# Weights in three groups, the first image's rows ahead of them, and new turn strings in a sixteen-image, four-block kernel

## The chip, the cores and the metric

The kernel runs on one core of a Trainium2 chip. The metric is the device time of one execution in microseconds (us). Before the change it was 2970.29 us, the median of three runs (2969.28 to 2974.66).

## The reference

Sixteen images of 256 rows by 128 features, all in float32, go through four branches one after the other. Each branch takes a layer norm of the image, scales and shifts it by rows of a modulation computed once from a condition vector, and adds its result back, for the first two branches and the second two times a gate row:

```
mod = (silu(c) @ wmod).reshape(16, 6, 1, 128)       # once for each of two layers
h = layernorm(x) * (1 + ca) + sa
x = x + ga * mamba(h)                 # branch a: conv of 4 taps, selective scan over 256 steps, 16 states
x = x + gb * routed(h2)               # branch b: 8 small experts, 2 chosen, and a shared one
x = x + ga1 * delta_rule(h3)          # branch c: 8 heads, gated delta rule over 256 steps
x = x + gb1 * attention_and_8_experts(h4)           # branch d
```

The images do not depend on each other. The weights are the same for all.

## The kernel before, in words

One image is too serial to fill the engines, so two are in work at a time. The steps of an image are split into a FIRST_HALF (x: branches a, b and the projections of c) and a SECOND_HALF (y: the pair products, the triangular inversion and the application of c, and branch d). `follow` writes, for each engine, first the whole first half of image 0, then a loop over i = 1 to 15 whose body holds the first half of image i and the second half of image i-1, and at the end the second half of image 15. In the loop body the order of the steps on each engine is a string of x and y, one string for each of TensorE (PE), VectorE (DVE), ScalarE (ACT) and GpSimd (POOL), in the table TURNS: each letter takes the next step of that half which this engine has. The engines run their own rows in order and meet through semaphores; a step that waits holds back everything behind it on its engine.

The steps that the change and the prediction speak of, with their lines in the kernel before:

- First half, branch a. `a_norm`/`a_norm2`: layer norm (DVE L1211 to L1223, one power on POOL L513). `a_turn`: transpose on PE (L797) and scale and shift on ACT (L602). `a_in`: the two input products (PE L808, L811), copied by ACT (L607, tanh L609). `a_conv`: 4 taps on DVE (L1278, L1281). `a_zgate` (L1271), `a_silu2` (L1286), `a_xproj` (PE L817, L819; ACT L618, L619), `a_split` (DVE L1291 to L1300), `a_dt` (PE L826), `a_soft` and `a_step` (DVE L1306 to L1315, ACT L623, L625). Then the scan in 8 groups: `a_scan` st is a spread of B and C on PE (L832), 4 exponentials on ACT (L637), the product `drive` (DVE L1324) and the scan itself (DVE L1336); `a_read` st is the product with C (DVE L1344), a sum on POOL (L535) and a product that adds up on PE (L855). `a_out` is the output product (PE L861), `a_res` the residual (DVE L1232, L1234).
- Second half, pair products: four groups of `c_logd` (PE L960, L961, ACT L704) and two `c_prod` (PE L970, DVE L1484, L1486); POOL builds `c_gmask` (L555). Then the inversion: `c_first` (DVE L1494), and five levels of `lev_T` (DVE L1500, L1503), `lev_Z` (PE L978, DVE L1507), `lev_TT` (PE L978, ACT L715), each for two chunks of the image. Then its application (`c_top`, `c_low`, `c_X` and so on), branch d, and its experts `d_up` (PE L1141, ACT L762), `d_down` (PE L1151) and `d_mix` (DVE L1632).

In the program's names, `wide` and `small` hold branch a's values, `mats` and `inv` the pairs and the inversion, `pad` the padded rows of a convolution, `banks` is PSUM, where products land.

Before the first image there is a prologue. SyncE (SP) issues all 43 weight loads with one semaphore, `loaded` (L450). All other engines wait for all of it. Then ACT and DVE make silu(c), PE makes the modulation from it (L780, L783), DVE turns it into `shift_scale` (L1179, L1182) and into gate rows (L1188 to L1200), SP stores the gate rows to DRAM (L452), waits for that, and only then loads the first image (L456) and the gate rows spread over the partitions (L459).

## Time and profile before

| what | value |
|---|---|
| median of 3 runs | 2970.29 us |
| the profiled execution's own time | 2970.33 us |
| its span, first to last instruction | 2968.5 us |
| PE busy | 2431.9 us, 82% |
| DVE busy | 2207.0 us, 74% |
| ACT busy | 1202.5 us, 41% |
| POOL busy | 650.6 us, 22% |
| mean granted TensorE clock | 0.907 of 2.4 GHz |

In the timeline, the pair stage of the loop starts at 201.94 us for image 1, at 377.56 and at 555.19 us for the next ones, so a pass of the loop takes some 177.6 us. A pass can be read in stretches of a few microseconds: what the engines do there, how much of it they are busy, and which of them is waited for. A total over the span hides these.

### The profile page before, as it was taken

The numbers are of one execution on the slowest core, as the hardware profiler recorded it, in microseconds if no ns is written. First come the engines' busy times: TensorE is split into PE (matmuls) and PEld (weight loads), VectorE is DVE, ScalarE is ACT, GpSimd is POOL, SyncE is SP. The second block draws the span as 40 slices with busy tenths as digits, with TensorE's granted clock in tenths as the row PEclk, the third lists the DMA queues.
The fourth block names the chain that finished last, engine by engine and source line by source line (L and its number), as shares of the span: only waits on it lengthen the run. The fifth ranks groups of instructions, "written<-read, shape, count | busy, mean of one in ns | idle before, by whom it ended". The sixth has DMA issues, their size and how long they took to land.

```text
span 2968.5 us, 60546 instructions
## 1 busy us (share of the span) xinstructions
PE 2431.9 (82%) x22424; PEld 1916.4 (65%) x22424; DVE 2207.0 (74%) x5056; ACT 1202.5 (41%) x2697; POOL 650.6 (22%) x465
## 2 busy tenths in 40 slices
PE   1478878979887897978889887887988789798897
PEld 1166766757666585756757676675866667576685
DVE  1668777787977778787787877778697777878752
ACT  0333532435344253533525353343534425353432
POOL 0222122131212212122132212213121221312110
PEclk9569989989899998989989998998989899898999
DMA  4000000000000000000000000000000000000000
GB/s 125 2 2 3 1 7 3 7 3 7 2 3 7 3 7 3 1 8 2 8 3 7 2 3 7 3 7 3 7 2 3 7 3 7 3 3 5 1 6 2
DMA packets 24830, 21.39 MB, mean 7 GB/s; under 512 B 7217, under 2 KB 21570, under 8 KB 24530
## 3 DMA queue, kind: packets, MB, share of 16 engines
q1 hardware_dynamic: 24530, 17.26, 2.1%
q8 instruction: 204, 3.34, 0.5%
q14 instruction: 96, 0.79, 0.1%
HBM read 15.13 MB, written 2.13 MB: 6 GB/s over the span
## 4 chain that ended last, share of the span: by engine, by line
PE 42%; issue 27%; DVE 23%; POOL 5%; ACT 2%; SPq 1%; DMA 1%; DVEq 0%; POOLq 0%; ACTq 0%
PE banks L978 6%; PE banks L1151 4%; PE banks L1004 4%; PE banks L1141 4%; PE banks L855 4%; DVE wide L1336 3%; PE banks L970 3%; DVE wide L1324 3%; DVE wide L1344 2%; PE banks L996 2%; PE banks L918 2%; PE banks L960 2%; POOL lg L539 2%; DVE inv L1507 2%; PE banks L927 2%
## 5 line engine op out<-in xcount | busy, mean ns | idle before, releaser
L535 POOL TENSOR_TENSOR wide<-wide 128x512 f32<-128x512 f32 x128 | 260.2, 2033 | 861.0 <-DVE wide L1344 543.5
L1456 DVE SCALAR_TENSOR_TENSOR wide<-pad,conv,wide 128x256 f32<-128x256 f32 x864 | 368.6, 494 | 0.0
L637 ACT ACTIVATE wide<-small,a_neg 128x255 f32<-128x255 f32 x512 | 217.7, 496 | 188.0 <-DVE wide L1336 187.9
L1336 DVE TENSOR_TENSOR_SCAN wide<-wide 128x1024 f32<-128x1024 f32 x128 | 291.6, 2278 | 1.9 <-ACT wide L637 0.3
L762 ACT ACTIVATE inv<-banks,up1b 128x256 f32<-128x256 f32 x512 | 212.1, 489 | 126.6 <-PE banks L1141 126.4
L1141 PE MATMUL banks<-inv,up 128*128 128x256 f32 x1024 | 262.3, 387 | 0.0
L1151 PE MATMUL banks<-down,inv 128*128 128x128 f32 x2048 | 258.9, 277 | 0.0
L1151 PEld LDWEIGHTS banks<-down,inv 128*128 128x128 f32 x2048 | 248.7, 192 | 5.0
L832 PE MATMUL banks<-bc,sel3b 96*128 96x256 bf16 x512 | 110.4, 323 | 162.5 <-DVE wide L1344 134.3
L978 PE MATMUL banks<-inv 64*64 64x64 f32 x5120 | 200.9, 237 | 48.1 <-DVE inv L1507 44.3
L978 PEld LDWEIGHTS banks<-inv 64*64 64x64 f32 x5120 | 184.8, 151 | 73.7 <-issue 73.6
L996 PE MATMUL banks<-hideb,identb 128*128 128x512 bf16 x640 | 207.2, 408 | 0.0
L978 PE MATMUL banks<-inv,mats 64*64 64x64 f32 x5120 | 186.3, 229 | 11.0 <-DVE inv L1500 6.6
L978 PEld LDWEIGHTS banks<-inv,mats 64*64 64x64 f32 x5120 | 174.2, 144 | 32.5 <-issue 30.0
L832 PEld LDWEIGHTS banks<-bc,sel3b 96*128 96x128 bf16 x512 | 45.0, 111 | 230.8 <-DVE wide L1344 149.9
L1141 PEld LDWEIGHTS banks<-inv,up 128*128 128x128 f32 x1024 | 181.2, 190 | 19.4
L715 ACT COPY inv<-banks 128x512 f32<-128x512 f32 x160 | 92.7, 579 | 216.5 <-DVE inv L1503 199.9
L1324 DVE TENSOR_TENSOR wide<-banks,small 128x1024 f32<-128x1024 f32 x128 | 154.0, 1203 | 7.7 <-PE banks L832 7.6
L513 POOL TENSOR_TENSOR vscale<-vscale,expo 128x16 f32<-128x16 f32 x16 | 46.3, 2896 | 512.1 <-DVE rq L1465 512.1
L1344 DVE TENSOR_TENSOR wide<-banks,wide 128x1024 f32<-128x1024 f32 x128 | 154.9, 1210 | 1.1
L602 ACT ACTIVATE hT_x<-banks,shift_scale 128x256 f32<-128x256 f32 x48 | 27.1, 565 | 295.3 <-PE banks L797 295.3
L927 PEld LDWEIGHTS banks<-ones_col,wide 128*128 128x128 f32 x1024 | 137.4, 200 | 14.2 <-issue 8.2
(277 smaller groups left out, 4966.3 us busy)
## 6 DMA issues: line engine op xcount, KB each, us to landing
gates_bc<-gate_rows SPq DMA_DIRECT2D x32, 128.0 KB, 2.9
up<-in_W SPq DMA_DIRECT2D x1, 2048.0 KB
x<-in_x SPq DMA_DIRECT2D x16, 128.0 KB, 2.2
out<-xn_y SPq DMA_DIRECT2D x16, 128.0 KB, 2.1
wide<-in_wmod SPq DMA_DIRECT2D x2, 384.0 KB
con<-in_con SPq DMA_DIRECT2D x1, 724.0 KB
w_k<-in_Wk SPq DMA_DIRECT2D x1, 512.0 KB
w_q<-in_Wq SPq DMA_DIRECT2D x1, 512.0 KB
```

What stands on the lines that cost most here:

```text
L535: g.tensor_tensor(ypart[p % 2], r[:, 0:512], r[:, 512:1024], ALU.add).then_inc(a_yp.h, 1)
L637: last = s.activation(decay[st % 2][:, at + 1:at + T], dt[:, c, 1:T], ACT.Exp, scale=a_neg[:, c, st * SG + q:st * SG + q + 1])
L762: s.activation(hm[e % 2][:, m, :], bank(3 + half, T, q * T), ACT.Relu, bias=up1b[:, HB1 * e + m:HB1 * e + m + 1]).then_inc(d_hid.h, 1)
L927: last = t.matmul(bank(2, 1, (kind * TILES + ch) * NH + m), sq[m % 2][:, kind, ch * P:(ch + 1) * P], ones_col[:], start=True, stop=True)
L978: last = t.matmul(PS[a:b, out, h * HALF:(h + 1) * HALF], weights(h, a, b), values(h, a, b), start=True, stop=True)
L996: t.matmul(bank(bk), identb[:], hideb[:].unsqueeze(1).broadcast_to([P, HG, P]), start=True, stop=True)
L1141: last = t.matmul(bank(3 + half, T, q * T), up1[:, e, m * P:(m + 1) * P], xxT, start=True, stop=True)
L1151: last = t.matmul(bank(bk, D, j * D), hm[e % 2][:, m, j * P:(j + 1) * P], down1[:, HB1 * e + m, :], start=m == 0, stop=m == HB1 - 1)
L1324: v.tensor_tensor(drive[st % 2].rearrange("p (q c t) -> p q c t", q=SG, c=CB), bank(0).rearrange("p (q t) -> p q t", t=T).unsqueeze(2).bro ...
L1336: v.tensor_tensor_scan(state[st % 2], decay[st % 2], drive[st % 2], 0.0, ALU.mult, ALU.add).then_inc(a_h.h, 1)
L1344: v.tensor_tensor(r, bank(1).rearrange("p (q t) -> p q t", t=T).unsqueeze(2).broadcast_to([P, SG, CB, T]), r, ALU.mult).then_inc(a_rd.h, 1)
L1456: v.scalar_tensor_tensor(dst, src, w, dst, ALU.mult, ALU.add).then_inc(c_conv.h, 1)
```

## The change

Weights come in three groups with a semaphore each: `loaded` (the condition, the constants and the modulation's weights, and between them, with its own semaphore, the first image), `loaded_first` (what the first steps of branch a need) and `loaded_late` (the rest, the larger part). Each engine waits for the group it needs at the place where it needs it: PE waits for `loaded_late` ahead of image 0's `a_out`, DVE ahead of its `a_res`, ACT ahead of its first `c_proj`. The gate rows are computed after the first image's layer norm, and POOL's memsets stand ahead of its wait. The four turn strings are other ones.

```diff
-    "tensor": ("yyyyyyyyyyyyxxyyyyyyxyyxyyyyyyxxxyxxyyxxyyyyxx...
+    "tensor": ("yyyyyxyxyyyyyyxyyxyyyyyyyyxyyyyxxxxyyxxyyyxyyx...
...
-            (con[:], a["con"]), (cT[:, 0, :], a["c0T"]), (cT[:, 1, :], a["c1T"]),
+            (cT[:, 0, :], a["c0T"]), (cT[:, 1, :], a["c1T"]), (con[:], a["con"]),
             (wmod[:, 0, :], a["wmod0"]), (wmod[:, 1, :], a["wmod1"]),
+        ]
+        loads_first = [
...
+            for dst, src in loads[:2]:
+                sp_.dma_start(dst, src).then_inc(loaded, 16)
+            load_x(0)
+            for dst, src in loads[2:]:
+                sp_.dma_start(dst, src).then_inc(loaded, 16)
+            for dst, src in loads_first:
+                sp_.dma_start(dst, src).then_inc(loaded_first, 16)
+            for dst, src in loads_late:
+                sp_.dma_start(dst, src).then_inc(loaded_late, 16)
             sp_.wait_ge(prep_dve, 12)
             sp_.dma_start(gates_dram, gates[:]...).then_inc(gates_stored, 16)
             sp_.wait_ge(gates_stored, 16)
-            load_x(0)
             load_gates(0, 0, gx_loaded)
...
             s.activation(xc[:, 0, 0:2 * NB]..., cT[:], ACT.Exp, scale=-1.0).then_inc(silu_c, 1)
+            s.wait_ge(loaded_first, LOADED_FIRST)
...
-            s.wait_ge(prep_dve, 12)
+            s.wait_ge(prep_dve, 8)
...
-            t.wait_ge(prep_dve, 12)
-            t.wait_ge(prep_act, 7)
             t.wait_ge(prep_pool, 1)
+            t.wait_ge(loaded_first, LOADED_FIRST)
...
+            def a_norm2(i):
+                norm2(i, 0)
+                if isinstance(i, int):
+                    modulation()
+                    gate_rows()
```

On DVE, in the prologue and the first steps of image 0, these rows stand in a row before, where `shift_scale` and `gates` are the modulation, `stats_x` and `mv_x` the layer norm:

```order
L1177 TENSOR_TENSOR cT<-cT,small 128x32
L1179 COPY shift_scale<-banks 128x128
L1182 TENSOR_SCALAR shift_scale<-shift_scale 128x16 x4
L1188 TENSOR_SCALAR inv<-banks 16x512
L1189 TENSOR_SCALAR inv<-banks 16x512
L1191 TENSOR_SCALAR inv<-banks 16x512
L1194 TENSOR_TENSOR inv<-inv 16x512
L1195 TENSOR_SCALAR inv<-inv 16x512
L1197 TENSOR_TENSOR gates<-inv 16x512
L1200 TENSOR_SCALAR gates<-gates 16x128
L1211 BN_STATS stats_x<-x 128x6 x2
```

and these now (L1239 to L1251 are the layer norm, L1206 the copy of the modulation):

```order
L1200 TENSOR_TENSOR cT<-cT,small 128x32
L1239 BN_STATS stats_x<-x 128x6 x2
L1241 COPY carried<-con 128x1
L1243 BN_AGGR mv_x<-stats_x 128x2 x2
L1245 TENSOR_SCALAR mv_x<-mv_x 128x2
L1251 TENSOR_SCALAR xn_x<-x,mv_x 128x128 x2
L1206 COPY shift_scale<-banks 128x128
L1209 TENSOR_SCALAR shift_scale<-shift_scale 128x16 x4
L1217 TENSOR_SCALAR inv<-banks 16x512
L1218 TENSOR_SCALAR inv<-banks 16x512
```

The layer norm has moved ahead of the modulation's copy, while PE makes the modulation; the gate rows stay between it and image 0's convolution.

On PE, in the pair stage of the loop, the end of the stage was (L960, L961 is a `c_logd`, each L970 pair a `c_prod`, L797 `a_turn`, L808 and L811 `a_in`):

```order
L957 REGISTER_ALU
L960 MATMUL banks<-inv,con 128x512
L961 MATMUL banks<-hideb,identb 128x512
L967 REGISTER_ALU
L970 MATMUL banks<-kq 128x256 x2
L967 REGISTER_ALU
L970 MATMUL banks<-kq 128x256 x2
L795 ISA
L797 MATMUL banks<-con,xn_x 128x128 x2
L808 MATMUL banks<-hT_x,w_in 128x256 x2
L811 MATMUL banks<-hT_x,w_in 128x256 x2
L982 ISA
```

and the second of the four groups is now (L983, L984 for `c_logd`, L993 for `c_prod`, L817 for `a_turn`, L828 and L831 for `a_in`):

```order
L980 REGISTER_ALU
L983 MATMUL banks<-inv,con 128x512
L984 MATMUL banks<-hideb,identb 128x512
L990 ISA
L993 MATMUL banks<-kq 128x256 x2
L815 ISA
L817 MATMUL banks<-con,xn_x 128x128 x2
L990 REGISTER_ALU
L993 MATMUL banks<-kq 128x256 x2
L828 MATMUL banks<-hT_x,w_in 128x256 x2
L831 MATMUL banks<-hT_x,w_in 128x256 x2
L980 REGISTER_ALU
```

The transpose and the input products of the new image have moved from behind the four groups to between the second and the third. On DVE the convolution has moved with them, from behind `c_first` and the first `lev_T` to behind the second group's products; `a_zgate` follows the third group, and `a_silu2` stands ahead of `c_first`.

On PE, in the inversion, the spread of B and C for the first scan group (L832) stood behind the fourth level's `lev_Z`, and in its last row here it waits for the first `drive`:

```order
L978 MATMUL banks<-inv 64x64 x32
L982 REGISTER_ALU
L978 MATMUL banks<-inv,mats 64x64 x16
L982 REGISTER_ALU
L978 MATMUL banks<-inv,mats 64x64 x16
L838 ISA
L839 REGISTER_ALU
L832 MATMUL banks<-bc,sel3b 128x256 x4
L845 ISA
L832 MATMUL banks<-bc,sel3b 128x256 x4
```

Now it stands one level earlier (L852 is the spread, L1001 the inversion, and an x32 row a level's `lev_TT` for both chunks):

```order
L1005 REGISTER_ALU
L1001 MATMUL banks<-inv,mats 64x64 x16
L1005 REGISTER_ALU
L1001 MATMUL banks<-inv,mats 64x64 x16
L858 ISA
L859 REGISTER_ALU
L852 MATMUL banks<-bc,sel3b 128x256 x4
L865 ISA
L852 MATMUL banks<-bc,sel3b 128x256 x2
L1001 MATMUL banks<-inv 64x64 x32
L1005 REGISTER_ALU
L1001 MATMUL banks<-inv,mats 64x64 x16
```

Behind the spread and its wait there is a whole level of the inversion now that stood ahead of it. From the fourth scan group to the experts, the rows are nearly where they were; among the experts, a few projections of branch c change places with experts' products, and DVE's fourth `d_mix` stands behind three more of its convolutions.

## Rows read from the trace of the kernel before

**Rows 1.** The page: span, PE, DVE, and the code queue

```profile
span 2968.5 us, 60546 instructions
...
PE 2431.9 (82%) x22424; PEld 1916.4 (65%) x22424; DVE 2207.0 (74%) x5056; ACT 1202.5 (41%) x2697; POOL 650.6 (22%) x465
...
q8 instruction: 204, 3.34, 0.5%
```

**Rows 2.** The DMA view of 0 to 60 us: GB/s in 40 slices

```profile
GB/s 0 232 306 277 332 225 107 222 299 254 373 157 10 8 165 109 42 176 399 377 402 304 288 291 291 244 0 0 0 0 0 0 0 0 15 7 149 113 0 0
```

**Rows 3.** Timeline, start: start us, us, engine, line, work [idle before]

```profile
39.71 0.23 ACT L586 ACTIVATE small<-cT 128x32 f32<-128x32 f32 x1 [37.69 <-DMA down1b<-in_b]
...
46.83 0.29 DVE L1179 COPY shift_scale<-banks 128x128 f32<-128x128 f32 x1 [5.57 <-PE banks L783]
...
51.25 0.21 DVE L1200 TENSOR_SCALAR gates<-gates 16x128 f32<-16x128 f32 x1
...
53.08 0.40 SPq L456 DMA_DIRECT2D x<-in_x  x1
...
55.43 0.49 DVE L1211 BATCH_NORM_STATS2 stats_x<-x 128x6 f32<-128x128 f32 x2 [3.96 <-DMA x<-in_x]
...
58.82 0.56 ACT L602 ACTIVATE hT_x<-banks,shift_scale 128x256 f32<-128x256 f32 x1 [17.99 <-PE banks L797]
```

**Rows 4.** The same view, DVE from 60 us

```profile
62.17 0.74 DVE L1278 TENSOR_SCALAR small<-pad,conv,conv0b 128x256 f32<-128x256 f32 x2 [4.28 <-ACT pad L607]
...
124.51 0.42 DVE L1232 TENSOR_TENSOR xn_x<-banks,gates_bc 128x256 f32<-128x256 f32 x1 [1.25 <-PE banks L861]
```

**Rows 5.** Stretches of one pass: us, busy (x), clock, DMA

```profile
560.60:573.20 12.60, 11.64 (x43) 7.92 (x41) 8.15 (x31) 2.39 (x4) 5.07 (x9) 0.93 0.07 21
573.20:599.50 26.30, 22.43 (x474) 18.48 (x474) 22.04 (x44) 10.89 (x19) 0.49 (x1) 0.94 0.01 3
599.50:621.90 22.40, 13.14 (x214) 10.36 (x215) 22.30 (x21) 11.23 (x27) 8.36 (x3) 0.70 0.01 1
697.00:705.00 8.00, 7.97 (x53) 7.15 (x52) 7.12 (x18) 6.71 (x16) 0.00 (x0) 1.00 0.01 2
```

**Rows 6.** Timeline of DVE in that pass, from the pairs on

```profile
573.14 0.89 DVE L1223 TENSOR_SCALAR xn_x<-x,mv_x 128x128 f32<-128x128 f32 x2
...
578.00 0.70 DVE L1278 TENSOR_SCALAR small<-pad,conv,conv0b 128x256 f32<-128x256 f32 x2
578.61 2.46 DVE L1281 SCALAR_TENSOR_TENSOR small<-pad,conv,small 128x256 f32<-128x256 f32 x6
...
583.64 0.65 DVE L1271 SCALAR_TENSOR_TENSOR small<-small,banks 128x512 f32<-128x512 f32 x1
...
588.90 0.29 DVE L1291 CAST bc<-small 96x256 bf16<-96x256 f32 x1 [1.97 <-ACT rank_sb L619]
...
621.89 2.28 DVE L1336 TENSOR_TENSOR_SCAN wide<-wide 128x1024 f32<-128x1024 f32 x1
```

**Rows 7.** Timeline of PE, the same stretch

```profile
574.08 0.44 PE L797 MATMUL banks<-con,xn_x 128*128 128x128 f32 x2 [1.84 <-DVE xn_x L1223]
575.32 1.44 PE L808 MATMUL banks<-hT_x,w_in 128*128 128x256 f32 x4 [0.80 <-ACT hT_x L602]
576.55 1.91 PE L811 MATMUL banks<-hT_x,w_in 128*128 128x256 f32 x4
...
606.93 1.97 PE L978 MATMUL banks<-inv 64*64 64x64 f32 x32
...
620.65 1.15 PE L978 MATMUL banks<-inv 64*64 64x64 f32 x32 [0.68 <-DVE inv L1507]
```

**Rows 8.** Timeline, experts: a late mix and its product

```profile
714.76 0.60 DVE L1632 SCALAR_TENSOR_TENSOR inv<-banks,gt,inv 128x128 f32<-128x128 f32 x2
...
722.76 1.05 PE L1151 MATMUL banks<-down,inv 128*128 128x128 f32 x8
```

More of the change, by code:

```diff
@@ L324, in build @@
         gm = sb("gm", [P, 4])
-        loaded = sem("weights_loaded")
+        loaded = sem("modulation_loaded")
+        loaded_first = sem("first_half_loaded")
+        loaded_late = sem("late_weights_loaded")
         mod_done = sem("modulation_products")
@@ L421, in build @@
             (at_b[:], a["fb"]), (gate_w[:], a["fWg"]), (gate_b[:], a["fbg"].partition_broadcast(P)),
+            (up1b[:], a["b1"]),
+            (down1b[:], a["b2"]),
             (up1[:], a["W1"].rearrange("e d f -> d e f")),
-            (up1b[:], a["b1"]),
             (down1[:], a["W2"].rearrange("e (m p) d -> p (e m) d", p=P)),
-            (down1b[:], a["b2"]),
         ]
-        LOADED = 16 * len(loads)
+        LOADED, LOADED_FIRST, LOADED_LATE = 16 * len(loads), 16 * len(loads_first), 16 * len(loads_late)
         def follow(eng, turns, steps):
@@ L448, in _ @@
         def _(sp_):
-            for dst, src in loads:
-                sp_.dma_start(dst, src).then_inc(loaded, 16)
-            sp_.wait_ge(prep_dve, 12)
-            sp_.dma_start(gates_dram, gates[:].rearrange("b n d -> b (n d)")).then_inc(gates_stored, 16)
-            sp_.wait_ge(gates_stored, 16)
             def load_x(i):
@@ L503, in _ @@
                 g.memset(cf[:, n, 8:9], 1.0)
+            g.wait_ge(loaded, LOADED)
             g.tensor_copy(identb[:], ident)
@@ L542, in c_gate @@
             def c_gate(i):
+                if isinstance(i, int):
+                    g.wait_ge(prep_act, 7)
                 g.wait_ge(c_gv.h, c_gv.at(i, 1))
@@ L663, in c_proj @@
                 at = m
+                if m == 0 and isinstance(i, int):
+                    s.wait_ge(loaded_late, LOADED_LATE)
                 if m < 9:
@@ L857, in a_out_ @@
             def a_out_(i):
+                if isinstance(i, int):
+                    t.wait_ge(loaded_late, LOADED_LATE)
                 t.wait_ge(a_ys.h, a_ys.at(i, 2))
@@ L1177, in _ @@
             v.tensor_tensor(cT[:], cT[:], ec, ALU.mult).then_inc(prep_dve, 1)
-            v.wait_ge(mod_done, 1)
-            v.tensor_copy(shift_scale[:].rearrange("p n b -> p (n b)"), bank(4, 8 * NB)).then_inc(prep_dve, 1)
-            v.wait_ge(prep_dve, 4)
-            for n in range(4):
-                v.tensor_scalar(shift_scale[:, 2 * n + 1, :], shift_scale[:, 2 * n + 1, :], 1.0, None, ALU.add).then_inc(prep_dve, 1)
-            g4 = PS[0:NB, 5, :]
-            sgn = inv[0:NB, 0]
-            mag = inv[0:NB, 1]
@@ L1196, in _, with modulation @@
-            v.wait_ge(silu_c, 5)
-            v.tensor_tensor(gates[:].rearrange("b n d -> b (n d)"), sgn, mag, ALU.mult).then_inc(prep_dve, 1)
-            v.wait_ge(prep_dve, 11)
-            v.tensor_scalar(gates[:, 0, :], gates[:, 0, :], 0.5, None, ALU.mult).then_inc(prep_dve, 1)
-            v.wait_ge(prep_dve, 12)
-            v.wait_ge(prep_act, 7)
-            v.wait_ge(prep_pool, 1)
+            v.wait_ge(prep_pool, 1)
+            def modulation():
+                v.wait_ge(mod_done, 1)
+                v.tensor_copy(shift_scale[:].rearrange("p n b -> p (n b)"), bank(4, 8 * NB)).then_inc(prep_dve, 1)
+                v.wait_ge(prep_dve, 4)
+                for n in range(4):
+                    v.tensor_scalar(shift_scale[:, 2 * n + 1, :], shift_scale[:, 2 * n + 1, :], 1.0, None, ALU.add).then_inc(prep_dve, 1)
@@ new lines, in gate_rows @@
+            def gate_rows():
+                g4 = PS[0:NB, 5, :]
+                sgn = inv[0:NB, 0]
+                mag = inv[0:NB, 1]
+                neg = inv[0:NB, 2]
+                v.tensor_scalar(sgn, g4, 0.0, 2.0, ALU.is_ge, ALU.mult).then_inc(prep_dve, 1)
+                v.tensor_scalar(mag, g4, -1.0, -0.25, ALU.mult, ALU.min).then_inc(prep_dve, 1)
+                v.wait_ge(prep_dve, 10)
+                v.tensor_scalar(neg, g4, -0.25, None, ALU.min).then_inc(silu_c, 1)
+                v.wait_ge(silu_c, 3)
+                v.tensor_tensor(mag, mag, neg, ALU.min).then_inc(silu_c, 1)
+                v.tensor_scalar(sgn, sgn, 1.0, -1.0, ALU.subtract, ALU.mult).then_inc(silu_c, 1)
+                v.wait_ge(silu_c, 5)
+                v.tensor_tensor(gates[:].rearrange("b n d -> b (n d)"), sgn, mag, ALU.mult).then_inc(prep_dve, 1)
+                v.wait_ge(prep_dve, 11)
+                v.tensor_scalar(gates[:, 0, :], gates[:, 0, :], 0.5, None, ALU.mult).then_inc(prep_dve, 1)
+                v.wait_ge(prep_dve, 12)
+                v.wait_ge(prep_act, 7)
@@ L1355, in a_res @@
             def a_res(i):
+                if isinstance(i, int):
+                    v.wait_ge(loaded_late, LOADED_LATE)
                 v.wait_ge(a_out.h, a_out.at(i, 1))
@@ L1637, in d_res @@
                 residual(i, 3, yacc)
-            follow(v, TURNS["vector"], dict(a_norm=lambda i: norm(i, 0), a_norm2=lambda i: norm2(i, 0), a_conv=a_conv_, a_zgate=a_zgate,
+            follow(v, TURNS["vector"], dict(a_norm=lambda i: norm(i, 0), a_norm2=a_norm2, a_conv=a_conv_, a_zgate=a_zgate,
                            a_silu2=a_silu2, a_split=a_split_, a_soft=a_soft1, a_step=a_step, a_scan=a_scan, a_read=a_read, a_y=a_y_, a_res=a_res,
```

42 lines of the change are left out of this document (20 added, 22 removed).

## The prediction, written before the run

> **What bounds the kernel now.** I read the page first, then the start as a timeline, then one pass of the loop in stretches, and last the same pass as timelines of DVE and PE. The page [rows 1] gives a span of 2968.5 us with PE busy 82% of it and DVE 74%. Neither is full, so the kernel is a sequence of stretches with different limits, and the change touches two of them.
>
> The first is the start. The reader is to see in [rows 3] that ACT's first real instruction starts at 39.71, after 37.69 us idle, released by the last weight to land (`down1b`). Nothing computes before that. The DMA view [rows 2] shows transfers up to the 26th slice of 1.5 us, that is to 39.0. After the weights come, in a row, the modulation (its copy on DVE at 46.83), the gate rows (ending at 51.25 + 0.21 = 51.46), their store, the first image's load (issued 53.08, read 55.43), the layer norm, ACT's scale and shift at 58.82, and the first convolution at 62.17 [rows 4].
>
> The second is the part of each loop pass from the pair products to the scan [rows 5]. While the pairs are made (560.6 to 573.2) PE is busy 11.64 of 12.60 us and DVE 8.15: PE sets the pace and DVE idles 4.45. In the inversion (573.2 to 599.5) neither is full: DVE is busy 22.04 of 26.30, idle 4.26; PE 22.43. In the first four scan groups (to 621.9) DVE is busy 22.30 of 22.40, PE only 13.14 at a granted clock of 0.70. Among the experts (697 to 705) PE is busy 7.97 of 8.00, and there the order of its rows hardly matters.
>
> **The start, step by step.** New first group: the two conditions, the image, the constants and the modulation's weights, 16 + 128 + 724 + 768 = 1636 KB, 1.68 MB. By the rates in [rows 2], 1.5 us a slice, 0.35 MB have moved at 3.0 us, 0.81 at 4.5, 1.22 at 6.0 and 1.72 at 7.5, so 1.68 at 7.4. The last traffic before the release at 39.71 is in the slice that ends at 39.0, so some 0.7 us lie between the last byte and the release: the group is there at 8.1. From the release to the end of the gate rows it was 51.46 - 39.71 = 11.75 us. That chain stays. The layer norm is put into DVE's wait for the modulation's products, 5.57 us of idle before 46.83 [rows 3], and costs about 2 us, so it is covered. ACT's scale and shift then start right behind `shift_scale`, about 46.83 + 0.7 - 39.71 = 7.8 us after the release, and the convolution came 62.17 - 58.82 = 3.35 after that step: 11.2. The gate rows on DVE, at 11.75, are a little later and decide. The convolution of image 0 starts at 8.1 + 11.75 + 0.1 = 20.0 in place of 62.17: 42.2 us earlier. I take 42.
>
> What could eat it: ACT waits for the second group behind its first activation. That group is 12 transfers and 0.55 MB more, 2.2 MB in all, which the rates of [rows 2] reach at 10.5; with 0.7, 11.2. ACT is needed only at 8.1 + 7.8 = 15.9, so this wait is hidden with 4.7 us in hand. The third group is as late as before, some 40. Its first user, `a_out`, whose product DVE reads at 124.51 [rows 4], comes at about 82 now: hidden by 40 us. The gate rows are stored when SP has issued all weights, some 40, and are read at the same 82. No row shows when a group of these transfers alone would land. The bounds: at the best rate of [rows 2], 332 GB/s, after an empty first slice, 1.5 + 5.1 + 0.7 = 7.3; at the mean of the first 60 us, 9.26 MB or 154 GB/s, 1.5 + 10.9 + 2.35 (the image's own issue to read, 53.08 to 55.43) = 14.8. So the start gives 35 to 43, nearest to the slices' own rates, 42. Everything behind the convolution up to the first loop pass keeps its order.
>
> One rule is to be weighed. The profile's code queue moved 204 packets, 3.34 MB, in 0.5% of 16 engines' span: 0.005 x 16 x 2968.5 / 204 = 1.16 us each [rows 1], and in the first 60 us the only queue with traffic was that of the weights. The Trainium skill (Runtime: NRT & Kernel Launch, Instruction fetch mechanics) says that each engine refills its instruction memory in blocks of 16 KiB over a DMA queue of its own, mostly hidden. In the changed kernel the first refills fall among the weights. By the rule as it stands the sum is unchanged; if two of them were waited for at the packet's 1.16 us the start would give 40.
>
> **A loop pass, step by step.** Moved into the pair stage on PE: `a_turn` 0.44, `a_in` 1.44 + 1.91 [rows 7], 3.79 us. PE paces this stage, so it gets 3.79 longer, and the inversion starts that much later. Moved on DVE from behind the pairs into them: normalising 0.89, convolution 0.70 + 2.46, `a_zgate` 0.65 [rows 6], 4.70 us. DVE has 4.45 + 3.79 = 8.24 idle there to hold them. `a_silu2` stays on the path ahead of `c_first`. So the stretch behind the pairs loses 4.70 of DVE's work, and at the same idle time a pass gains 4.70 - 3.79 = 0.91.
>
> The rest hangs on DVE's 4.26 idle in the inversion [rows 5]. The largest piece is 1.97 us before L1291, released by ACT's `rank_sb` [rows 6]: `a_xproj` stood on PE behind two levels' products. Now it runs while DVE does `c_first` and the first transposes, and that wait goes: 0.91 + 1.97 = 2.88. The other 2.29 are waits for PE's products, partly filled by the steps that now lie between. Against this stands a new wait. PE's spread for the first scan group stands a level earlier and waits for the first `drive` on DVE. Queued behind it on PE are a `lev_TT` and the next `lev_Z`, and DVE waits for these, though it has a scan of 2.28 us to do meanwhile. And PE, idle more in between, may run them at half clock: 1.97 us for 32 products in place of 1.15 [rows 7], 0.82 each, four such on the chain at most. I take half of one, 0.4, since DVE's scans cover most, which gives 2.5 us a pass. The bounds: all idle used, 0.91 + 4.26 = 5.2; none used and four slow steps on the path, 0.91 - 3.3 = -2.4. Where scan group 5 starts (621.89 [rows 6]) nearly the old order is reached, so the gain is carried on: PE is full from there, and its next work waited for the inversion.
>
> Among the experts the fourth `d_mix` (714.76) moves behind three convolution steps, 6.5 us, to 721.3. PE's product at 722.76 [rows 8] needs it: 1.4 in hand. I cost this at 0, up to 1 us a pass if the convolutions run late. `a_turn`'s counterpart of branch c, moved ahead of the first expert, is worth at most the few tenths that PE idles there: 0.
>
> 15 passes x 2.5 = 37.5. The second half of image 15 has no partner and keeps its order. The profiled execution took 2970.33 us, 1.8 more than its span, and stands at the median of 2970.29. Sum: 2970.3 - 42 - 37.5 = 2890.8, so 2891.
>
> **The rivals.**
>
> (1) Only the start pays. The freed DVE time was hidden, a pass stays within half a microsecond. For it: in the scan stretch DVE is full (22.30 of 22.40), and whatever makes the scan ready earlier only pays if the inversion is ready too. Against it: the idle DVE time at the pairs is real and is the thing the new order fills. Time: 2970.3 - 42 = 2928.
>
> (2) The order pays nearly in full, 4.5 us a pass, the waits for PE being filled too: 2970.3 - 42 - 68 = 2860.
>
> (3) The transfers don't come in the order of issue. If all 43 are served side by side, the first group lands with the last, near 39, and the start gives only the reordering, 62.17 - 39.7 - 11.85 = 10.6. For it: no row shows one group alone. Against it: SP's issues take 0.4 us each while the traffic of [rows 2] rises and falls with what was issued. Time: 2970.3 - 10.6 - 37.5 = 2922.
>
> (4) Slower than before. Place: the pair stage on PE. If DVE's moved work had been covered by waits for PE anyway, its leaving gives nothing, and PE's 3.79 us is a plain loss in each pass: 2970.3 - 42 + 15 x 3.79 = 2985. It decides from a loss of 42 / 15 = 2.8 us a pass. Against it: DVE's rows from 573.14 to 585 stand nearly without a gap, so they were not covered.
>
> **How the numbers follow.** My forecast 0.60, rival (1) 0.18, (2) 0.12, (3) 0.05, (4) 0.04, and 0.01 for a loss in the loop that just cancels the start. The range from 2862 to 2930 holds the forecast's bounds for all but its ends, rival (1) and a part of (3). Under 0.2%, 6 us, a measurement of this kernel can't be told from no change: faster 0.95, same 0.01, slower 0.04.
>
> **What would show it.** In the changed kernel's profile, DVE's first modulation copy should stand near 15.2 and the first convolution near 20; if it stands near 50, rival (3) holds. PE's first matmul should be near 10. DVE must show no wait for `loaded_late`, neither at image 0's `a_res` nor elsewhere. In a pass, the pair stage should be 16 to 17 us long in place of 12.6, with DVE idle about 3.5 in it; the wait before the first cast of `a_split` (1.97) should be gone; and pass to pass it should be 175 us against 177.6. The forecast is wrong in the loop if the stretch from the pairs' end to scan group 5, 48.7 before, is not at least 4 us shorter, or if what is gained there comes back as idle PE before the experts.

## The result and the profile after

The changed kernel takes 2872.94 us (median of four runs, 2863.03 to 2874.62), the kernel before, measured beside it, 2969.78 (2960.30 to 2974.66). The ratio is 0.9671, 95% interval 0.9638 to 0.9704: 3.3% faster. The forecast was 2891, range 2862 to 2930.

Both profiled executions lie within 1.5 us of their medians, so the difference of the spans, 2968.5 - 2872.6 = 95.9 us, can be laid out along the program. The marks are the first `c_gmask` on POOL of each pass (the pair stage's first instruction):

| part | before | after | difference | forecast |
|---|---|---|---|---|
| start, to the first pair stage | 201.94 | 159.98 | -41.96 | -42 |
| 15 passes of the loop, mean | 175.93 | 172.39 | -3.54 each, -53.1 in all | -2.5 each, -37.5 |
| from the last pass to the end | 127.6 | 126.8 | -0.8 | 0 |

The 177.6 us a pass that stood ahead of the prediction was one pass; the mean of the 15 is 175.93.

The page of the changed kernel, the rows that answer to [rows 1]:

```profile
span 2872.6 us, 60547 instructions
PE 2416.6 (84%) x22424; PEld 1916.6 (67%) x22424; DVE 2214.2 (77%) x5056; ACT 1202.6 (42%) x2697; POOL 654.9 (23%) x465
q8 instruction: 204, 3.34, 0.5%
```

The work is the same, in a shorter span. The DMA view of its first 60 us, in 40 slices of 1.5 us:

```profile
GB/s 0 39 287 341 345 323 133 34 105 222 186 129 378 317 58 86 148 38 60 183 408 404 382 315 291 289 291 209 1 103 72 5 0 0 0 0 0 5 0 0
```

Against [rows 2] the second slice is nearly empty (39 for 232): SP issued the constants, 724 KB, first at 0.74 before, and now at 2.12, behind the two conditions and the image. After that the traffic has much the same height and ends some 3 us later, at 42 for 39. The transfers as a whole were not sped up; only who waits for which has changed. The timeline of the changed kernel's start (start us, us, engine, line, work, and in brackets the idle time before and what ended it):

```profile
8.90 0.23 ACT L603 ACTIVATE small<-cT 128x32 f32<-128x32 f32 x1 [6.88 <-DMA wide<-in_wmod]
10.18 0.48 DVE L1239 BATCH_NORM_STATS2 stats_x<-x 128x6 f32<-128x128 f32 x2
10.40 3.56 PE L801 MATMUL banks<-cT,wide 128*128 128x16 f32 x16 [10.40 <-DVE cT L1200]
12.88 0.23 ACT L605 ACTIVATE a_neg<-a_neg 128x32 f32<-128x32 f32 x1 [3.75 <-DMA up0b<-in_up0b]
15.82 0.29 DVE L1206 COPY shift_scale<-banks 128x128 f32<-128x128 f32 x1 [3.21 <-PE banks L804]
16.74 0.56 ACT L620 ACTIVATE hT_x<-banks,shift_scale 128x256 f32<-128x256 f32 x1 [2.86 <-DVE shift_scale L1209]
20.25 0.21 DVE L1229 TENSOR_SCALAR gates<-gates 16x128 f32<-16x128 f32 x1
20.50 0.73 DVE L1312 TENSOR_SCALAR small<-pad,conv,conv0b 128x256 f32<-128x256 f32 x2
28.49 10.49 SPq L477 DMA_DIRECT2D gate_rows<-gates  x1
83.53 0.42 DVE L1266 TENSOR_TENSOR xn_x<-banks,gates_bc 128x256 f32<-128x256 f32 x1 [1.37 <-issue]
```

The group of the modulation's weights releases ACT at 8.90, where it was 39.71 [rows 3]. The second group costs ACT a wait of 3.75 us, to 12.88, but ACT then waits for `shift_scale` anyway. The convolution, the last row but two, was at 62.17 [rows 4]. The first `a_res` comes at 83.53 in place of 124.51 [rows 4], 41 us behind the end of the weights' traffic, with its idle time as before (1.37 against 1.25).

One pass of the changed kernel's loop, which starts at 503.26, is shown next. It is 170.84 long, one of the shortest (mean 172.39), and starts at full clock, where the pass of [rows 5] starts at 0.79 and takes 175.80; so single stretches show the shape, and the means of the table below the size. Its stretches (us long; busy us of PE, its weight loads, DVE, ACT, POOL; granted clock; DMA share, GB/s):

```profile
508.60:523.30 14.70, 12.40 (x51) 8.55 (x49) 13.52 (x42) 4.95 (x9) 5.58 (x9) 1.00 0.09 19
523.30:541.60 18.30, 13.99 (x336) 11.71 (x336) 16.27 (x29) 8.39 (x15) 0.00 (x0) 1.00 0.01 3
541.60:566.30 24.70, 17.32 (x330) 13.83 (x332) 24.46 (x23) 9.09 (x21) 7.88 (x4) 0.79 0.01 2
627.20:674.10 46.90, 46.90 (x316) 43.16 (x315) 38.34 (x112) 35.28 (x83) 7.17 (x4) 1.00 0.00 1
```

The first is the pair stage: 12.60 us before [rows 5], 14.70 now, and DVE fills 13.52 of it in place of 8.15. The second is the inversion up to the first scan group: 26.3 us before, 18.3 now. The scan stretch has more of the inversion in it and DVE is full there as before. The last is the experts' stretch, where PE is never idle. DVE in the same pass:

```profile
514.92 1.35 DVE L1312 TENSOR_SCALAR small<-pad,conv,conv0b 128x256 f32<-128x256 f32 x2 [0.60 <-ACT pad L625]
516.20 2.46 DVE L1315 SCALAR_TENSOR_TENSOR small<-pad,conv,small 128x256 f32<-128x256 f32 x6
520.27 0.67 DVE L1305 SCALAR_TENSOR_TENSOR small<-small,banks 128x512 f32<-128x512 f32 x1
523.57 2.79 DVE L1531 TENSOR_TENSOR inv<-mats,con 64x512 f32<-64x512 f32 x4
527.63 0.25 DVE L1325 CAST bc<-small 96x256 bf16<-96x256 f32 x1
565.22 2.28 DVE L1370 TENSOR_TENSOR_SCAN wide<-wide 128x1024 f32<-128x1024 f32 x1
```

and PE:

```profile
511.96 0.38 PE L817 MATMUL banks<-con,xn_x 128*128 128x128 f32 x2
513.18 1.09 PE L828 MATMUL banks<-hT_x,w_in 128*128 128x256 f32 x4
514.10 1.03 PE L831 MATMUL banks<-hT_x,w_in 128*128 128x256 f32 x4
541.91 0.39 PE L852 MATMUL banks<-bc,sel3b 96*128 96x256 bf16 x2 [1.94 <-DVE wide L1358]
546.13 2.89 PE L1001 MATMUL banks<-inv,mats 64*64 64x64 f32 x64 [1.82 <-DVE inv L1540]
553.41 3.68 PE L1001 MATMUL banks<-inv 64*64 64x64 f32 x64
```

Against [rows 6]: the first cast of `a_split` (L1325) has no wait, 1.97 before; scan group 5 (L1370) starts 61.96 into the pass, 66.70 before. Against [rows 7]: the transpose and the input products, now among the pairs, take 0.38 + 1.09 + 1.03 = 2.50 us in place of 3.79. The lower three rows are the price: waits of 1.94 for the first `drive` and of 1.82 for the inversion, and inversion products at half speed (3.68 for 64 of them; 2.08 in the row of 542.24). Half speed is not new there: before, 32 of them took 1.97 [rows 7].

The mean over the 15 passes of each kernel, as offsets from the pass's start:

| mark | before | after | difference |
|---|---|---|---|
| `c_first` on DVE | 18.11 | 21.03 | +2.92 |
| first `drive` | 43.63 | 38.29 | -5.34 |
| scan group 5 (the fifth of the eight scans) | 66.06 | 63.03 | -3.03 |
| branch d's residual before the experts (`d_xx`) | 126.53 | 123.96 | -2.57 |
| first DVE row behind `c_ba` | 131.26 | 127.77 | -3.49 |
| next pass | 175.93 | 172.39 | -3.54 |

### The profile page after: what moved, and what is told of

It is laid out like the page before. It is cut to its first block, busy times and chain, and to the rows that moved or that the text cites. A ratio compares the mean times of both kernels' runs of the same rounds, so it can differ in the third digit from the quotient of the medians.

```text
span 2872.6 us, 60547 instructions
## 1 busy us (share of the span) xinstructions
PE 2416.6 (84%) x22424; PEld 1916.6 (67%) x22424; DVE 2214.2 (77%) x5056; ACT 1202.6 (42%) x2697; POOL 654.9 (23%) x465
## 3 DMA queue, kind: packets, MB, share of 16 engines
q8 instruction: 204, 3.34, 0.5%
## 4 chain that ended last, share of the span: by engine, by line
issue 40%; PE 30%; DVE 19%; POOL 6%; ACT 1%; POOLq 0%; DVEq 0%; ACTq 0%
PE banks L1001 7%; PE banks L1027 4%; PE banks L875 3%; PE banks L993 3%; DVE wide L1370 2%; DVE wide L1358 2%; POOL lg L553 2%; DVE inv L1544 2%; PE banks L1019 2%; PE banks L852 2%; POOL rq L525 2%; DVE inv L1540 1%; PE banks L983 1%; PE banks L1049 1%; PE banks L1041 1%
## 5 line engine op out<-in xcount | busy, mean ns | idle before, releaser
L1370 DVE TENSOR_TENSOR_SCAN wide<-wide 128x1024 f32<-128x1024 f32 x128 | 292.9, 2289 | 1.9 <-ACT wide L655 0.3
L1001 PE MATMUL banks<-inv,mats 64*64 64x64 f32 x5120 | 186.1, 234 | 52.9 <-DVE inv L1540 34.5
L1001 PEld LDWEIGHTS banks<-inv,mats 64*64 64x64 f32 x5120 | 176.0, 148 | 71.1 <-issue 69.7
L1001 PEld LDWEIGHTS banks<-inv 64*64 64x64 f32 x5120 | 183.6, 152 | 53.1 <-issue 52.2
L1001 PE MATMUL banks<-inv 64*64 64x64 f32 x5120 | 196.0, 239 | 25.2 <-DVE inv L1544 22.6
L852 PE MATMUL banks<-bc,sel3b 96*128 96x256 bf16 x512 | 107.1, 314 | 113.5 <-DVE wide L1378 77.2
L852 PEld LDWEIGHTS banks<-bc,sel3b 96*128 96x128 bf16 x512 | 41.9, 108 | 176.7 <-DVE wide L1378 92.4
L1669 DVE SCALAR_TENSOR_TENSOR inv<-banks,gt,inv 128x128 f32<-128x128 f32 x256 | 76.3, 345 | 97.7 <-PE banks L1174 95.8
L993 PE MATMUL banks<-kq 128*128 128x256 f32 x512 | 138.8, 414 | 7.2 <-DVE mats L1523 7.1
```

The lines of the kernel that those rows point to most:

```text
L852: last = t.matmul(bank(bk, T, q * T), sel3b[:, row + q:row + q + 1].broadcast_to([3 * 2 * NS, P]), bc3[:], start=True, stop=True)
L993: last = t.matmul(bank(3 + n % 2, 256, y * 256), kq[:, h, 0, ch * P:(ch + 1) * P], kq[:, h, :, ch * P:(ch + 1) * P], start=True, stop=True)
L1001: last = t.matmul(PS[a:b, out, h * HALF:(h + 1) * HALF], weights(h, a, b), values(h, a, b), start=True, stop=True)
L1370: v.tensor_tensor_scan(state[st % 2], decay[st % 2], drive[st % 2], 0.0, ALU.mult, ALU.add).then_inc(a_h.h, 1)
```

## The experiments

In all of them "starts" is the first pair stage, "pass" the mean of the 15 passes, and the marks are those of the table above. A part of the turn strings that is taken from one kernel or the other moves steps without altering the work. Where not said otherwise a time is the median of four runs, beside seven of the kernel before on the same chip.

### The two parts alone

The loads alone, with the strings of before:

```diff
-    "tensor": "yyyyyxyxyyyyyyxyyxyyyyyyyyxyyyyxxxxyy...
+    "tensor": "yyyyyyyyyyyyxxyyyyyyxyyxyyyyyyxxxyxxy...
(the strings of the other three engines too)
```

> The changed kernel with the turn strings of before: only the weights' groups and the earlier image. Theory A (start and loop are separate and add up): the first pair stage begins near 160.0 as in the changed kernel (201.94 before), a pass takes 175.9 as before, total 2969.8 - 42 = 2928. Theory B (the earlier start also changes what the passes do, by the clock or the transfers): a pass differs from 175.9 by 0.5 us or more, total off 2928 by 8 or more.

Measured: 2926.99 us, ratio 0.9862 (0.9841 to 0.9884). Starts at 161.1, pass 175.77, tail 128.8. The start alone is worth its 41 us and does not touch a pass.

The strings alone, the loads of before:

```diff
-    "tensor": "yyyyyyyyyyyyxxyyyyyyxyyxyyyyyyxxxyxxy...
+    "tensor": "yyyyyxyxyyyyyyxyyxyyyyyyyyxyyyyxxxxyy...
(the strings of the other three engines too; nothing of the loads)
```

> The kernel before with the new turn strings: only the order in the loop. Theory A: start as before (pairs at 201.9), a pass takes 172.4, total 2969.8 - 53 = 2917. Theory B (a part of the loop's 53 us comes from the earlier start): a pass takes 173 or more, total above 2925.

Measured: 2914.75 us, 0.9838 (0.9808 to 0.9867). Starts at 201.8, pass 172.20. The two parts add up: (1 - 0.9862) + (1 - 0.9838) = 3.0%, against 3.3% together, within the intervals.

### The strings in halves

The new strings to the scan's end, those of before behind it (branch c's projections among the experts); on DVE:

```diff
-...xxxyxxxyyyxxxyyyxyxxxyxxxyxyxxxxxyxxyyyyy
+...xxxyxxxyyyxxyxyyxyxxxxxyxxyyxxyxxxxxyyyyy
```

> The changed kernel, each engine's turn string new up to the scan's end and as before behind it. Theory A (two gains: pairs to scan 2.5 us a pass, the earlier transpose and first products of branch c 1.0): a pass takes 173.4, total 2873 + 15 = 2888. Rival (all of it is due to the pairs and the scan, and the last 1.0 us is theirs, since PE gets to the experts in another state): a pass 172.4, total 2873.

And the other half:

```diff
-    "vector": "xyxyyyxyyxyyxyyyyxyyxyyyyyyxyyxyyxxxyy...
+    "vector": "xyyyyyyyyxyyyyxyyyxyxyyxyyxyyyyxyxyxxy...
```

> The changed kernel, each engine's turn string as before up to the scan's end and new behind it. Theory A: a pass takes 174.9, total 2928 - 15 = 2913. Rival (the late part pays only behind the early one): a pass 175.9, total 2928.

Measured: the first 2899.93 us, 0.9772 (0.9753 to 0.9792), pass 174.01, scan group 5 at 63.67. The second 2917.07, 0.9833 (0.9813 to 0.9853), pass 175.14, and `d_xx` to `c_ba` 3.80 in place of 4.72. Neither theory had the first one; the second lies near the first theory (174.9 and 2913), though its `d_xx` stands 0.3 later than with the loads alone. With the early half new, scan group 5 is early by 2.4, but the pass is only 1.76 shorter than with the loads alone. So the late half, costed at nothing, carries a part, and it does so at one place, 0.92 between `d_xx` and `c_ba`. The halves don't add up to the whole: 1.76 + 0.63 = 2.4 of 3.4 us (175.77 - 172.39). What is odd in the two kernels is told below, as far as the traces show it.

Branch c's projections (`c_proj`, `c_turn_k`, `c_turn_v`) as before, `c_turn` and `c_ba` at their new places, and the early half new; on PE:

```diff
-...xxyxyxyyyxyyxyyxyyxyyyxxyyyyyxyyxyyxyyxyyxyyyxyxyyxyxyyyyxyxyx
+...xxyxyxyyyxyyxyyxyyyxyyxyyyyxyyxyxyyxyyxyyxyyyxyxyyxyyxxyyyyyxx
```

> The changed kernel with branch c's projections (c_proj, c_turn_k, c_turn_v, c_scales) at the places of before; new up to c_soft2, so that branch c's transpose and its first products (c_turn, c_ba) stand ahead of the first expert's second half as in the changed kernel. Theory T (the last 1.0 us of a pass is the earlier c_turn and c_ba): a pass 172.4, total 2873, within 5. Rival (the shuffled projections carry it): a pass 173.3, total 2887.

Measured: 2882.76 us, 0.9719 (0.9699 to 0.9738), pass 172.69, `d_xx` to `c_ba` 3.80. In the trace that is the theory's side: the place of `c_turn` and `c_ba` gives the 0.92, the other projections 0.3 (172.69 - 172.39). Its total lay between the two expectations, 2873 and 2887. The rows of before and of after at that place show it. Before, PE and then DVE:

```profile
682.60 1.11 PE L1141 MATMUL banks<-inv,up 128*128 128x256 f32 x4
683.54 0.38 PE L797 MATMUL banks<-con,xn_x 128*128 128x128 f32 x2
685.55 0.38 PE L1121 MATMUL banks<-con,gt 128*8 128x128 f32 x2 [0.33 <-DVE gt L1619]
685.77 0.52 PE L904 MATMUL banks<-w_ba,hT_x 128*128 128x16 f32 x4
```

```profile
681.59 0.48 DVE L1600 SCALAR_TENSOR_TENSOR inv<-banks,at_b,hT_y 128x256 f32<-128x256 f32 x1 [2.10 <-PE banks L1108]
686.32 0.19 DVE L1417 COPY bax<-banks 128x32 f32<-128x32 f32 x1 [0.83 <-PE banks L904]
```

and after, PE and then DVE:

```profile
625.47 0.38 PE L817 MATMUL banks<-con,xn_x 128*128 128x128 f32 x2
626.68 1.11 PE L1164 MATMUL banks<-inv,up 128*128 128x256 f32 x4
627.63 0.51 PE L927 MATMUL banks<-w_ba,hT_x 128*128 128x16 f32 x4
```

```profile
624.39 0.60 DVE L1251 TENSOR_SCALAR xn_x<-x,mv_x 128x128 f32<-128x128 f32 x2 [0.81 <-POOL mv_x L525]
625.68 0.48 DVE L1637 SCALAR_TENSOR_TENSOR inv<-banks,at_b,hT_y 128x256 f32<-128x256 f32 x1 [0.68 <-PE banks L1131]
629.49 0.18 DVE L1454 COPY bax<-banks 128x32 f32<-128x32 f32 x1
```

DVE's normalising of the next image (L1251) stands ahead of `d_xx` now, in the idle time there (2.10 before), and the transpose on PE ahead of the first expert. `c_ba`'s product (L904, now L927) stood behind the expert's second half and a product that waits 0.33 for DVE's `gt`, 4.18 us behind the start of `d_xx`; now it comes 1.95 behind it, and DVE finds it ready.

### The early half in its three steps

Only the pair stage new (and the late half), the scan's lead-in as before:

```diff
-    "tensor": "yyyyyxyxyyyyyyxyyxyyyyyyyyxyyyyxxxxyyxxyyyx...
+    "tensor": "yyyyyxyxyyyyyyxyyyyyyyyxyyyyyyxxxyxxyyxxyyy...
-    "vector": "xyxyyyxyyxyyxyyyyxyyxyyyyyyxyyxyyxxxyyxxyyx...
+    "vector": "xyxyyyxyyxyyxyyyyyyyyyyxyyxyyyyxyxyxxyxxyxy...
```

> The changed kernel with the new places of branch a's steps only up to a_xproj (those that lie among the pairs); a_split to the scan's end stand where they stood before; everything behind the scan is new. Theory P (the gain up to the scan is the pair stage's idle time, filled): scan group 5 starts 1.8 us earlier in a pass than the 66.05 of before, which leaves 173.6 a pass, total 2891. Rival S (the pair stage only trades PE's time for DVE's, and what pays is that the scan's first groups stand a level earlier): scan group 5 at most 0.5 us earlier, a pass 174.9, total 2911.

Measured: 2899.31 us, 0.9778 (0.9760 to 0.9797), pass 173.93, first `drive` at 42.71, scan group 5 at 65.13. Against the second half-and-half kernel that is 0.94 earlier at scan group 5 and 1.21 a pass: close to the 0.91 of the prediction, and between the two expectations (1.8 and at most 0.5 earlier). The wait ahead of the first cast is gone in this kernel too (0.00 us).

The pair stage and the steps up to `a_dt` and `a_step` new as well, the scan itself where it was, a level of the inversion later:

```diff
-    "tensor": "yyyyyxyxyyyyyyxyyxyyyyyyyyxyyyyxxxxyyxxyyyx...
+    "tensor": "yyyyyxyxyyyyyyxyyxyyyyyyyyyyyyxxxyxxyyxxyyy...
-    "vector": "xyxyyyxyyxyyxyyyyxyyxyyyyyyxyyxyyxxxyyxxyyx...
+    "vector": "xyxyyyxyyxyyxyyyyxyyxyyyyyyxyyyyyxyxxyxxyxy...
```

> As the run before, but a_split, a_dt, a_soft and a_step stand at their new places too; only the scan and its reads stand where they stood before. Theory P: nearly all of the gain is there, scan group 5 at 63.5, a pass 172.9, total 2880. Rival S: as without, 174.5 or more, total 2905.

Measured: 2908.99 us, 0.9805 (0.9786 to 0.9824), pass 174.54, first `drive` at 43.03, scan group 5 at 65.46. The wait ahead of the cast is gone (0.06 us in the mean, 1.97 before), and nothing is won by it: the rival's side. Two of its 15 passes take 177.40 and 179.38; the others behind the first take 174.0 to 174.3, as most of the kernel above do. Why these two are longer is open. DVE in the pass that starts at 506.27:

```profile
531.80 0.25 DVE L1325 CAST bc<-small 96x256 bf16<-96x256 f32 x1
538.64 0.69 DVE L1544 TENSOR_TENSOR inv<-banks,con 128x512 f32<-128x512 f32 x1 [0.74 <-PE banks L1001]
545.63 0.72 DVE L1540 STREAM_TRANSPOSE inv<-banks 128x512 f32<-128x512 f32 x1 [0.73 <-PE banks L1001]
547.68 0.69 DVE L1544 TENSOR_TENSOR inv<-banks,con 128x512 f32<-128x512 f32 x1 [0.40 <-PE banks L1001]
549.01 1.22 DVE L1358 TENSOR_TENSOR wide<-banks,small 128x1024 f32<-128x1024 f32 x1 [0.64 <-PE banks L852]
```

The idle time stands now in pieces of 0.2 to 0.7 us ahead of the levels' products. With the steps early there is nothing left that DVE could put between two levels, unless the scan comes with them. The changed kernel is this one with the scan a level earlier: scan group 5 at 63.03, pass 172.39. The 1.97 was won only by the two together (65.13 to 63.03 at scan group 5; the scan can't go ahead of the steps that feed it). Some 0.4 of that 2.1 goes with the clock at a pass's start, told next: among the passes that start below full clock it is 65.43 to 63.74, 1.7.

### The clock at a pass's start

A pass starts at one of two speeds. Two passes of the kernel before, one of each, and then two of the kernel with only the early half new, each for its first 8 us:

```profile
730.99:738.99 8.00, 6.19 (x35) 4.64 (x34) 4.09 (x15) 1.39 (x4) 2.04 (x3) 1.00 0.18 51
906.14:914.14 8.00, 6.20 (x30) 4.61 (x29) 3.23 (x12) 1.38 (x3) 2.04 (x3) 0.79 0.17 51
```

```profile
856.43:864.43 8.00, 6.32 (x30) 4.64 (x29) 3.15 (x12) 1.38 (x3) 3.05 (x6) 0.79 0.19 54
1030.47:1038.47 8.00, 6.26 (x30) 4.58 (x29) 3.10 (x12) 1.38 (x3) 3.06 (x6) 0.79 0.19 53
```

At a granted clock of 1.00 all of these matmuls run at 2.4 GHz, at 0.79 a part at 1.2. Counted over the passes behind the first, which starts at 0.61 to 0.74 in every kernel:

| kernel | passes that start at 1.00 | their mean | the others' mean |
|---|---|---|---|
| before | 6 | 174.81 | 176.81 |
| only the loads new | 7 | 174.91 | 176.90 |
| only the late half new | 6 | 175.24 | 175.14 |
| only the early half new | 0 | - | 174.07 |
| only the pair stage new | 1 | 172.67 | 174.23 |
| after | 6 | 171.57 | 173.21 |

More than half of what a slow start costs stands already at the end of the pair stage: before, `c_first` is 17.60 into a pass that starts at full clock and 18.73 into the others, and in the changed kernel 20.33 and 21.78. With the early half alone these 14 passes are 174.0 to 174.2 long, every one with the same start. The changed kernel's passes that also start below full clock are 0.86 shorter (174.07 - 173.21), nearly the 0.92 of `c_ba`, and at scan group 5 the two are 0.09 apart (63.83 and 63.74). Another 0.70 goes with the six passes that start at full clock there (173.21, against 172.51 for all 14). So the first kernel's shortfall is the late half's gain, not yet there, and the clock with which passes begin. The sum of the halves is not closed by this: with the late half alone, passes of either start take the same (175.24 and 175.14), though `c_first` is 0.85 apart in them; they are level again at `d_xx` (126.82 and 126.72). This is a correlation over passes. Two runs tried to change it. Fill matmuls behind `c_decay`, the last product of the pass:

```diff
                 last.then_inc(c_dec.h, 1)
+                if not isinstance(i, int): keep_warm(5)
```

> The changed kernel with two more products without a use (0.43 us) at the end of each pass on PE, ahead of the branch. Theory K (the half clock that 8 or 9 of 15 passes start with costs 1.6 us each and hangs on how busy PE was before the branch): fewer passes start at 0.8, a pass is the same or up to 0.4 us shorter, total 2867 to 2873. Rival (the share of slow starts stays): each pass 0.43 longer, total 2879.

Measured: 2882.29 us, 0.9727 (0.9704 to 0.9751), pass 172.65, five passes at full clock. In this profile the fill, 0.43 us a pass, gave no more full starts (5 for 6), and the pass is 0.26 longer, not shorter: the theory fell, at this size of fill. The total is 3 us above even the rival's 2879. And fill in the scan, where PE idles most:

```diff
+                if st == 0 and not isinstance(i, int): keep_warm(7)
                 if st + 1 < NG:
...
             def a_read(i, st):
+                if st < 3 and not isinstance(i, int): keep_warm(7)
```

> The changed kernel with four pairs of products without a use (0.43 us each at full clock) on PE in a pass, in its waits for DVE during the first scan groups. Theory D (DVE is full there, so PE's clock costs nothing): the granted clock at 38 to 63 us of a pass rises from 0.78 to over 0.9 and a pass stays at 172.4 within 0.5. Rival (the half clock delays DVE's transposes and the applied chain behind it): a pass is 1 us or more shorter, total under 2860. A third way: the fills stand ahead of work that DVE waits for, a pass gets longer by up to 1.7 us.

Measured: 2888.93 us, 0.9731 (0.9715 to 0.9747), pass 173.66, scan group 5 at 64.39. In the stretch of one pass from 38 to 63 us the clock reads:

```profile
544.24:569.24 25.00, 17.07 (x298) 13.03 (x293) 23.99 (x23) 11.07 (x26) 7.44 (x3) 0.86 0.01 1
```

0.86 for 0.78 in the mean of the changed kernel, not the full clock, and the scan is 1.4 us later. A pass is 1.27 longer, the third way of the expectation, and two passes start at full clock. DVE is busy 23.99 of 25.00 there, against 24.76 in the same stretch of the changed kernel's pass shown above: it has little idle time for a faster PE to fill, and the fills hold it up. What the clock alone would give is not separated from what the fills cost.

### The order of the transfers

The constants (`con`) behind the modulation's weights, with a semaphore that only POOL waits for:

```diff
-            (cT[:, 0, :], a["c0T"]), (cT[:, 1, :], a["c1T"]), (con[:], a["con"]),
+            (cT[:, 0, :], a["c0T"]), (cT[:, 1, :], a["c1T"]),
...
+            for dst, src in loads_con:
+                sp_.dma_start(dst, src).then_inc(loaded_con, 16)
...
-            g.wait_ge(loaded, LOADED)
+            g.wait_ge(loaded_con, LOADED_CON)
```

> The changed kernel with the constants (724 KB) taken out of the first group and issued behind the image, with a semaphore of their own for which only POOL waits. Theory F (transfers land in the order of issue at the rates of the DMA view): the first group is 0.8 MB and lands at 6.4 in place of 8.9, and the first pair stage begins 2 to 2.5 us earlier, near 157.7. Rival (the transfers are served side by side, or something else sets the 8.9): it begins within 0.5 us of 160.0.

Measured once: 2872.96 us; starts at 158.08. The timeline of its start:

```profile
5.84 0.23 ACT L604 ACTIVATE small<-cT 128x32 f32<-128x32 f32 x1 [3.82 <-DMA wide<-in_wmod]
7.05 3.57 PE L802 MATMUL banks<-cT,wide 128*128 128x16 f32 x16 [7.05 <-DVE cT L1201]
18.55 0.73 DVE L1313 TENSOR_SCALAR small<-pad,conv,conv0b 128x256 f32<-128x256 f32 x2
```

Without the 724 KB of constants ahead of it, the modulation's group lands 3.06 us earlier (5.84 for 8.90), and the convolution comes 1.95 earlier; the rest goes to the layer norm, which now waits 4.61 us for POOL's copies of the constants. The same kernel again, timed in five runs, and beside it on the same chip the change itself:

> The kernel of the run before with the constants moved behind the modulation's weights, now timed beside the changed kernel on one chip. Its one profile had the first pair stage 1.9 us earlier than the changed kernel's (158.08 against 159.98) and loop passes of the same mean length. Theory F (transfers land in order of issue, so the start keeps the 1.9): 2871, ratio to the kernel before 0.9665. Rival (the 1.9 us are taken back by the clock with which the passes start): 2873 or more, not to be told from the changed kernel. The two are 0.07% apart, and a difference under 0.2% between the two totals decides nothing; the place of the first pair stage does: F has it at 158.1 again.

> The changed kernel itself, on this chip. Both theories: 2873 (2863 to 2882). It is the measure for the runs that differed from it in one part only: with c_turn and c_ba as in the kernel before (2883 measured on another chip) and with fill matmuls at the pass's end (2882). If it comes out at 2880 or over here, the 10 us by which those two stood above it were the chip's; at 2876 or under, they were the edits'. Passes that start at the full clock: theory of a fixed pattern has 6 of 15 again, the rival has another number.

Measured: 2875.94 us, 0.9688 (0.9669 to 0.9707), starts at 157.20, pass 172.67; and 2876.51 us, 0.9702 (0.9683 to 0.9720), starts at 160.71, pass 172.34. The start is 3.5 us earlier again (2.24 of it at the convolution, 18.03 against 20.27) and the totals are 0.57 apart, which no measurement here can tell from none. The rival's trade (the clock takes it back) is not shown either: 5 passes at full clock against 7, and against 6 in the change's first profile, is as much as the same kernel differs from itself. The change measured 2876.51 on this chip, between the marks that were to lay the 10 us of the two runs above (2882.76, 2882.29) on the chip (2880) or on their edits (2876), so that stays undecided; their ratios, 0.9719 and 0.9727, overlap with its own. (Of the first of these two the expectation says that it had `c_turn` and `c_ba` as in the kernel before; it had them at their new places, and only the projections as before.) No variant here is shown to beat the change.

## Why the prediction was right, point by point

**The start: right.** The steps stood at 8.1 for the group (8.90), near 10 for PE's first matmul (10.40), near 15.2 for the modulation's copy (15.82), 20.0 for the convolution (20.50), and the whole gained 41.96 for 42. The 0.5 to 0.8 too early came from the traffic's rise, a slice later than in [rows 2]. That the whole came within 0.04 is in part luck: the convolution moved by 41.67, and a second profile of the changed kernel has its first pair stage at 160.71, 41.2 earlier. Of the 41.67, 30.81 is the earlier release (39.71 to 8.90), and 10.86 is the image's load and the gate rows taken off the path; no run has one without the other. Rival (3) had all transfers land together; the order of issue holds, shown by the group at 8.90 and by the constants moved behind it (5.84). The wait for the second group was hidden, as said, and nothing waited for the third.

**The rule on instruction fetch.** The prediction took it that the first refills fall among the weights. They didn't. The DMA view of the first 60 us went from 11778 to 11780 packets, and the two more are code (q14, 0.02 MB), at 46.5 and 56.4 us, behind the weights; in the kernel before the first two of the span stand at 88.0 and 97.9. So each row of the start stands within 0.8 us of the sum that leaves fetches out, and the 40 us that two waited fetches would have left did not come, but no run here shows what a fetch among heavy traffic costs. The page (the Trainium skill, Runtime: NRT & Kernel Launch, Instruction fetch mechanics) has them mostly hidden, in blocks of 16 KiB. The size agrees, 3.34 MB in 204 packets or 16.4 KB each; the hiding was not put to the test.

**The loop: the direction and the main place right, the size too small, 3.54 for 2.5, and two gains credited to the wrong place.** By the prediction's own terms:

- The pair stage on PE: "3.79 us". `c_first` moved by 2.92. The moved matmuls' durations were taken at their old place, where the chain ran them partly at half clock (1.44 + 1.91 for the two input products in the pass read [rows 7], 1.44 + 1.59 in the mean of the 15); among the pairs they take 1.10 + 1.03 in the mean. This term was mis-sized by 0.87. With it DVE's idle time in the stage was 1.2 in this pass, not 3.5, and the stage 14.70 long, not 16 to 17.
- Behind the pairs: 4.70 + 1.97 - 0.4 = 6.27 less. From `c_first` to scan group 5 it was 47.96 and is 42.00, 5.96 less. The size is near. The attribution was not: the 1.97 were counted as won when the wait went, but two kernels without that wait (only the pair stage new; the steps new too) kept the time as small waits for the inversion's products. It was won when the scan, too, moved a level earlier, which the prediction had as a cost only. That the 0.31 is so small is luck.
- Scan group 5: -2.48 by these terms, -3.03 measured. The stretch from the pairs' end to there is 41.9 in the pass shown for 48.7, 6.8 shorter, against the "at least 4"; in the mean, from `c_first`, 5.96. It was carried on to the experts but for 0.46.
- Among the experts: "at most the few tenths that PE idles there: 0". It was 0.92 a pass. The error was to look only at PE's idle time. DVE had 2.10 idle ahead of `d_xx` and did its normalising for `c_turn` behind it, and on PE the product that starts branch c's gates stood behind the expert's second half and a product that waits for DVE; a busy PE hid that DVE's next row was late. The late fourth `d_mix` cost nothing that shows: that stretch has PE at 46.90 of 46.90.

Together 0.87 - 0.31 - 0.46 + 0.92 + 0.05 (behind `c_ba`) = 1.07 over the 2.48, which is the 3.54 within rounding.

**The rivals.** (1), only the start pays: the kernel with the loads alone is that case, 2926.99, and the strings alone gave 1.6%. (2), 4.5 a pass, is nearer to the total (2860) than the forecast by little: 12.9 off against 18. (4), the pair stage a plain loss: `c_first` is later, but all of DVE's 4.70 came back behind it.

**Open.** What sets whether a pass starts at full clock, and why that costs nothing with the late half alone. Fill at the pass's end (5 passes at full clock) and fill in the scan (2) did not raise the number above the changed kernel's 6. A run that keeps PE's activity the same over the whole pass was not tried.

## What to carry to other kernels

Split the weights by first use and issue them in that order: what stands ahead of the first computation is worth its landing time one for one, until the chain that is released becomes the limit. When a step is moved, price it at the clock of the stretch where it goes, not of the one where it stands. A wait that disappears is won only if what runs next has something ready; look for the next row that waits before counting it.
